# Cross-attention of a decoder layer: how the score maxima reach the rows of the queries

## What is computed

```python
q = (x @ Wq).reshape(B, N, HEADS, hd).transpose(0, 2, 1, 3)      # 16 heads of 32
k = (context @ Wk).reshape(B, M, HEADS, hd).transpose(0, 2, 1, 3)
v = (context @ Wv).reshape(B, M, HEADS, hd).transpose(0, 2, 1, 3)
scores = jnp.einsum('bhid,bhjd->bhij', q, k) * scale
scores = jnp.where(context_mask[:, None, None, :], scores, max_neg)
attn = jax.nn.softmax(scores, axis=-1)
out = jnp.einsum('bhij,bhjd->bhid', attn, v)
```

## Time and profile before

| | us |
|---|---|
| median of 3 runs | 3772.2 (3767.72 to 3776.98) |
| the profiled execution's own time | 3775.88 |
| its span, first to last instruction | 3774.1 |
| TensorE busy | 3639.7 (96%) |
| VectorE busy | 2361.0 (63%) |
| ScalarE busy | 1731.9 (46%) |
| GpSimd busy | 1305.9 (35%) |

### The profile page before, as it was taken

The page is one execution under the profiler, slowest core; times in us unless marked ns, Lnnn a source line. Parts: engine busy times, 40 slices in busy tenths (PEclk is TensorE's granted clock), DMA queues, the critical chain, the costliest instruction groups (busy, mean ns, idle before and its releaser), DMA issues. The chain is left out here.

```text
span 3774.1 us, 84215 instructions
## 1 busy us (share of the span) xinstructions
PE 3639.7 (96%) x28244; PEld 3139.7 (83%) x28244; DVE 2361.0 (63%) x5543; ACT 1731.9 (46%) x4278; POOL 1305.9 (35%) x1388
## 2 busy tenths in 40 slices
PE   8999999999979999999999999849999999999999
PEld 7888888888868888888888888638998899989998
DVE  6888888888846666666666666576433434434343
ACT  4555555555435555555555555413333333333332
POOL 2333333333325656666556566510101101011010
PEclk9999999999989999999999999869999999999999
DMA  4222222222243434444434343223324334234232
GB/s 127 60 54 63 54 63 53 64 53 64 72 122 94 112 106 104 108 116 107 121 96 113 104 108 97 71 68 94 121 82 122 107 98 123 82 118 123 85 108 69
DMA packets 315057, 349.72 MB, mean 93 GB/s; under 512 B 45308, under 2 KB 232036, under 8 KB 314884
## 3 DMA queue, kind: packets, MB, share of 16 engines
q1 hardware_dynamic: 305796, 318.26, 30.7%
q0 software_dynamic: 9088, 29.17, 2.4%
HBM read 183.23 MB, written 38.91 MB: 59 GB/s over the span
## 5 line engine op out<-in xcount | busy, mean ns | idle before, releaser
L1627 DVE TENSOR_REDUCE x_mx<-x_psS 112x1 f32<-112x752 f32 x512 | 479.7, 937 | 382.2 <-PE x_psS L1180 378.6
L2423 DVE TENSOR_TENSOR hid<-e_psU,act_g 128x280 f32<-128x280 f32 x256 | 115.1, 450 | 622.6 <-PE e_psU L34 585.8
L1462 ACT ACTIVATE x_pt<-x_psE 125x448 f32<-125x448 f32 x768 | 389.6, 542 | 227.6 <-PE x_psE L1192 217.7
L1051 POOL TENSOR_TENSOR part<-x_pt 125x448 f32<-125x448 f32 x255 | 292.4, 1147 | 506.0 <-ACT x_pt L1462 497.1
L2049 POOL DMA_INDIRECT out<-ex_y,sidx x40 | 39.8, 995 | 1020.4 <-DVE ex_y L2457 1010.2
L635 POOL TENSOR_TENSOR qks<-qks,cos 128x448 f32<-128x448 f32 x128 | 148.1, 1157 | 657.0 <-DMA qks<-qk 657.0
L1180 PE MATMUL x_psS<-k_st,q_st 97*112 97x376 f32 x1024 | 287.9, 362 | 24.1 <-DMA k_st<-mk 16.3
L32 PE MATMUL e_psG<-ex_hi,g_hi 128*128 128x280 f32 x1024 | 304.2, 297 | 6.7 <-ACT act_g L2208 4.5
L32 PE MATMUL pj<-xT_hi,win_hi 128*128 128x224 f32 x1024 | 302.2, 295 | 4.0 <-PEq L185 3.9
L2208 ACT ACTIVATE act_g<-e_psG 128x280 f32<-128x280 f32 x256 | 103.7, 405 | 426.4 <-PE e_psG L34 412.1
L1053 POOL TENSOR_TENSOR part<-part,x_pt 125x448 f32<-125x448 f32 x255 | 292.3, 1146 | 20.0
(11 more groups left out here) (305 smaller groups left out, 10890.3 us busy)
## 6 DMA issues: line engine op xcount, KB each, us to landing
k_st<-kT SPq DMA_DIRECT2D x768, 93.8 KB, 2.2
raw_g<-in_L_ffn_wg SPq DMA_DIRECT2D x128, 256.0 KB
raw_u<-in_L_ffn_wu SPq DMA_DIRECT2D x128, 256.0 KB
raw_d<-in_L_ffn_wd SPq DMA_DIRECT2D x128, 256.0 KB
qks<-qk SPq DMA_DIRECT2D x512, 56.0 KB, 2.0
q_st<-qT SPq DMA_DIRECT2D x384, 56.0 KB, 2.0
ctxt<-in_ctx SPq DMA_DIRECT2D x16, 1125.0 KB
xt<-in_x SPq DMA_DIRECT2D x16, 448.0 KB, 3.7
```

The lines of the kernel that those rows point to most:

```text
L1051: pool.tensor_tensor(part[:], pt[j][:, 0, :], pt[j][:, 1, :], ALU.add).then_inc(parted, 1)
L1462: act.activation(pt[j][:, i, :], psE[(j + i) % 2][0:KR, 0:2 * T], ACT.Exp, scale=XD ** -0.5).then_inc(exp_done, 1)
L1627: dve.tensor_reduce(mx[:, j, h:h + 1], psS[0:HT, :, 0:376], AX.XY, ALU.max).then_inc(s_taken, 1)
L2423: dve.tensor_tensor(h[ring][:, halves[s]], psU[:, 0:CH], act_g[i][:, halves[s]], ALU.mult).then_inc(S["mul"], 1)
```

## The change

VectorE splits the maxima where they stand (`split_max`), two instructions on 112 x 4 for a pair, right after `maximum` of its last head: a rounded negative high part, and the remainder. One transposition on TensorE turns the eight columns into 8 rows of 112. ScalarE copies them to m_row and issues a DMA from its own queue, which lays them down in rows 97 and 98 of q_st; it waits first for the previous one to land, and for its own copy. TensorE waits for the landing (m_placed) where it waited for the bank. Row 96 keeps the ones that an earlier stage wrote. Pair 0 moves from `first_gap` at j = 3 to the end of `second_gap` at j = 2, which on ScalarE is ahead of the exponentials of j = 3; pair 1 moves to the head of the next group, ahead of everything of it on TensorE and ScalarE. On VectorE the split of pair 0 comes before the residual and `low_k` at j = 1, that of pair 1 after the last maximum; `low_q(b, 3)` and `low_ctx(b, 2, 0)` move from after `maximum(3, 0)` to before it. Two short fills of GpSimd at the start go.

```diff
-UNITS = ("K10 V04 M1_0 K11 Q2 V05 Q3 M0_0 X0 X1 "
-         "K20 V10 M1_1 K21 V11 V12 V13 N0 M0_1 N1 O0 L "
-         "K30 M1_2 O1 K31 V14 V15 C00 C10 Q0 C20 M0_2 C01 Q1 C11 "
-         "K00 C21 V00 M1_3 K01 V01 V02 V03 M0_3").split()
+UNITS = ("M1_0 K10 V04 K11 Q2 V05 Q3 M0_0 X0 X1 "
+         "M1_1 K20 V10 K21 V11 V12 V13 N0 M0_1 N1 O0 L "
+         "M1_2 K30 O1 K31 V14 V15 C00 C10 Q0 C20 M0_2 C01 Q1 C11 "
+         "M1_3 K00 C21 V00 K01 V01 V02 V03 M0_3").split()
...
-            less = sb(c, "x_less", [P, 1])
+            m_parts, m_row = sb(c, "m_parts", [HT, 2, 8], F32R), sb(c, "m_row", [8, HT], F32R)
...
+            def max_placed(t, i):
+
+                return 32 * t + 16 * i + 16
+
+            fills = [ones[:]] + [k[96:99, :].bitcast(F32) for k in k_st]
...
                     def turn_max(u, t, i):
 
-                        pe.wait_ge(s_taken, 8 * t + 4 * i + 4)
+                        pe.wait_ge(m_split, 4 * t + 2 * i + 2)
                         o = bank(u)
-                        for n in range(4):
-                            m = pe.transpose(o[:, n * HT:(n + 1) * HT], mx[:, 2 * i + n // 2, n % 2:n % 2 + 1].to_broadcast((HT, P)),
-                                             ident[0:HT, 0:HT])
-                        m.then_inc(pj_full, 1)
+                        pe.transpose(o[0:8, 0:HT], m_parts[:, i, :].bitcast(F32), ident[0:HT, 0:HT]).then_inc(pj_full, 1)
...
                             elif j == 3:
-                                turn_max(U(f"M0_{g}"), n, 0)
                                 if g == 0 and not last:
...
-                                if prev:
-                                    turn_max(U(f"M1_{g}"), n - 1, 1)
                                 if g == 2 and not first:
                                     project_out(U("O1"), b - 1, 1)
...
                                 elif g == 3 and not last:
                                     project_v(U("V03"), 0, 3)
+                                turn_max(U(f"M0_{g}"), n, 0)
...
+                            if prev:
+                                turn_max(U(f"M1_{g}"), n - 1, 1)
                             for j in range(4):
                                 pe.wait_ge(k_placed[j], placed(b, g))
                                 scores(n, g, j, 0)
                                 if prev:
-                                    if j == 0:
-                                        done(U(f"M0_{gp}") if g else unit_of(b - 1, "M0_3"))
-                                    elif j == 2:
-                                        done(U(f"M1_{g}"))
+                                    if j in (0, 2):
+                                        pe.wait_ge(m_placed, max_placed(n - 1, j // 2))
                                     shifted(n - 1, gp, j, (0, 1))
...
-                    def high_max(u, g, i):
-
+                    def out_max(u, t, g, i):
+
+                        if i or not below(t, 1):
+                            act.wait_ge(m_placed, max_placed(t, i) - 16)
                         o = full(u)
-                        act.activation(q_st[96:99, 4 * g + 2 * i:4 * g + 2 * i + 2, :],
-                                       o[96:99, 0:2 * T].rearrange("p (j t) -> p j t", j=2), ACT.Identity,
-                                       bias=ident[96:99, 96:97], scale=ident[96:99, 98:99]).then_inc(m_high, 1)
+                        act.activation(m_row[:], o[0:8, 0:HT], ACT.Copy).then_inc(pj_free[u.bank], 1)
+                        act.wait_ge(pj_free[u.bank], u.after)
+                        head = 4 * g + 2 * i
+                        act.dma_start(q_st[97:99, head:head + 2, :].bitcast(F32), m_row[:].bitcast(F32)).then_inc(m_placed, 16)
...
                                 elif g == 3 and not last:
                                     out_v(U("V03"), 0, 3)
+                                out_max(U(f"M0_{g}"), t + g, g, 0)
...
                             n, prev = t + g, not (first and g == 0)
+                            if prev:
+                                out_max(U(f"M1_{g}"), n - 1, (g + 3) % 4, 1)
                             for j in range(4):
                                 if prev:
                                     exps(n - 1, j, range(3) if j == 3 else (0, 1))
...
-                    def low_max(u, n, g, i):
-
-                        dve.wait_ge(m_high, n)
-                        rows = q_st[96:99, 4 * g + 2 * i:4 * g + 2 * i + 2, :]
-                        dve.scalar_tensor_tensor(rows, pj[u.bank][96:99, 0:2 * T].rearrange("p (j t) -> p j t", j=2),
-                                                 less[96:99, 0:1], rows.bitcast(F32), ALU.mult, ALU.add).then_inc(pj_free[u.bank], 1)
+                    def split_max(t, i):
+
+                        raw, hi, lo = (mx[:, 2 * i:2 * i + 2, :], *(m_parts[:, i, k:k + 4].rearrange("p (j h) -> p j h", j=2) for k in (0, 4)))
+                        dve.wait_ge(s_taken, 8 * t + 4 * i + 4)
+                        dve.tensor_scalar(hi, raw, -1.0, None, ALU.mult).then_inc(m_split, 1)
+                        dve.wait_ge(m_split, 4 * t + 2 * i + 1)
+                        dve.scalar_tensor_tensor(lo, raw, -1.0, hi.bitcast(F32), ALU.mult, ALU.subtract).then_inc(m_split, 1)
...
-                                if g == 0:
-                                    low_q(b, 3)
                                 if pprev:
                                     out_y(n - 2, (g + 2) % 4, U("O1") if g == 2 and not first else None)
-                                if g == 2 and not last:
-                                    low_ctx(b, 2, 0)
-                                low_max(U(f"M0_{g}"), 2 * n + 1, g, 0)
...
                             elif j == 1:
+                                split_max(n, 0)
                                 if g == 2 and not first:
                                     residual(U("O1"), b - 1, 1)
...
                                 if g == 2 and not last:
                                     low_q(b, 0)
+                                if g == 0:
+                                    low_q(b, 3)
+                                elif g == 2 and not last:
+                                    low_ctx(b, 2, 0)
                             else:
+                                split_max(n, 1)
```

More of the change, by code:

```diff
@@ L966, in place_k @@
                         if below(t, 1):
-                            sp.wait_ge(zeroed, 1)
+                            sp.wait_ge(filled, len(fills))
                         for j in range(4):
@@ L1037, in _ @@
                 def _(pool):
[L1039 to L1042, removed]
+                    for n, f in enumerate(fills):
+                        pool.memset(f, 1.0).then_inc(filled, 1)
                         pool.wait_ge(filled, n + 1)
-                    pool.nop().then_inc(zeroed, 1)
                     def sum_blocks(t, g, heads=range(4)):
@@ L1235, in _ @@
                     pe.wait_ge(rw_out, 1)
-                    pe.wait_ge(zeroed, 1)
+                    pe.wait_ge(filled, len(fills))
                     pe.wait_ge(wo_loaded, 16)
@@ L1246, in first_gap @@
                         def first_gap(g, j):
-                            n, nxt, ng = t + g, not (last and g == 3), (g + 1) % 4
+                            nxt, ng = not (last and g == 3), (g + 1) % 4
                             if j < 2 and nxt:
@@ L1269, in second_gap @@
                         def second_gap(g, j):
-                            n, prev, pprev = t + g, not (first and g == 0), not (first and g < 2)
+                            n, pprev = t + g, not (first and g < 2)
                             if j == 0:
@@ L1350, in _ @@
                     n, last = 4 * B, lambda name: unit_of(B - 1, name)
-                    done(last("M0_3"))
+                    turn_max(last("M1_4"), n - 1, 1)
+                    pe.wait_ge(m_placed, max_placed(n - 1, 0))
                     shifted(n - 1, 3, 0, range(3))
-                    turn_max(last("M1_4"), n - 1, 1)
                     totals(n - 2, 2)
@@ L1357, in _ @@
                     turn_rows(last("N1_14"), B - 2, 1)
-                    done(last("M1_4"))
+                    pe.wait_ge(m_placed, max_placed(n - 1, 1))
                     shifted(n - 1, 3, 2, range(3))
@@ L1504, in first_gap @@
                             elif j == 3:
-                                high_max(U(f"M0_{g}"), g, 0)
                                 if g == 0 and not last:
@@ L1513, in second_gap @@
                         def second_gap(g, j):
-                            gp, prev = (g + 3) % 4, not (first and g == 0)
                             if j == 0:
@@ L1522, in second_gap @@
                                     out_v(U("V00"), 0, 0)
-                                if prev:
-                                    high_max(U(f"M1_{g}"), gp, 1)
                             elif j == 1:
@@ L1576, in _ @@
                     n = 4 * B
-                    exps(n - 1, 0, range(3))
```

(17 more changed lines are left out.)

8 lines of the change are left out of this document (4 added, 4 removed).

## The result

The kernel is slower. The changed kernel's median is 3823.3 us and the old one's, measured beside it, 3775.75, five runs each; the ratio is 1.0126, with a 95% interval of 1.0111 to 1.0141. One disturbed run of 4985.91 us is outside that ratio. The difference of the medians is 47.55 us, of the two profiled spans 45.9 (3774.1 and 3820.0). The forecast was 3809, by a sum of +37.2.

The account below looks back on a forecast made before the run. TensorE bounds the kernel, busy 1294.07 of 1320 us, with ScalarE without slack at j = 3. M0 +49.0, M1 -17.2 and VectorE +5.4 sum to +37.2 us: 3809 as a median, range 3768 to 3838.

Parts of the forecast that it names:

- The issue holds up ScalarE: Each maxima step adds 1.16 us on ScalarE, 0.82 of it DMA issue in which it can start nothing; chance 0.70.
- The rival of a free issue: Issue costs ScalarE nothing or under some 0.2 us: about -1 us, 3771, no measurable difference; chance 0.14.
- the dearer one: SyncE and ScalarE hold each other up, issue 1.21 us: +25 us, 3834; within the blocked queue's 0.70.
- The waits at j = 3: At a group's last head TensorE waits for ScalarE before the third pair, 0.6 to 1 us, some 60 times.
- M1 moved ahead: Pair 1's step at the next group's head: 0.23 us gained 63 times, plus a 2.7 us bank wait; -17.2 us.
- VectorE's moves: Two small VectorE operations of about 0.17 us each delay O1's residual; low_q and low_ctx moves mostly hidden; +5.4 us.
- V15: TensorE unit at g = 2, j = 1 taking its bank after the residual: 0.36 us later, 15 times, +5.4 us.
- The landing: ScalarE's rows land in 2.0 us, before TensorE wants them: no wait; rival of late landing 3863, chance 0.02.
- The term for M0: Pair 0's step ahead of the last head's exponentials delays TensorE 3.12 us a batch over 16 batches: +49.0 us.
- The faster rival: Issue free, removed TensorE transpositions gained: 27 us (3745), or 37 us if all 384 count (3735); chance 0.14.

Follow-up runs that it names:

- the run without it: Changed kernel with VectorE's split moved behind O1's residual: 3812.03 us, 11 us less than the changed kernel.

## Why the prediction was right in sign, and where its sum was off

- **The issue holds up ScalarE: right, and dearer than the rest of the step.** It takes 0.62 us where I took the mask row's 0.82; the exponentials start 1.03 us after the copy's start, not 1.16. As the copy also starts 0.10 us ahead of the recorded end of the instruction before it, the exponentials start 0.93 us after that (1773.35 - 1772.42), 0.23 less than the sum had. That accounts for the 0.2 us by which g = 0 came out below it, and for half of the 0.4 of g = 3. The rival of a free issue is out (in none of the 128 issues does ScalarE start an instruction), and so is the dearer one: 107 of the 128 run while SyncE issues too, and their median is 624 ns like that of the 21 others; a single one lasts 1.50 us. The Trainium skill (DMA: Bandwidth & Descriptors, "Issuing engines are not separate DMA queues") has the time to initiate a DMA as usually small against the DMA; 0.62 us of issue against the 2.0 us in which SyncE's mask row lands is not small, and on a compute engine with no slack it was two thirds of the 0.93; to move it alone gave back as much as to move the whole step.
- **The waits at j = 3: right.** Forecast were waits of 0.6 to 1 us some 60 times; there were 71 with 46.5 us in total, 0.92, 0.40, 0.82 and 0.55 us at the four groups of one batch.
- **M1 moved ahead: right per place.** A single transposition pushes TensorE on by 1777.49 - 1777.46 = 0.03 us where four took 0.31, so 0.28 each instead of 0.23.
- **"VectorE's moves": this step failed.** It looked at O1's residual and V15 alone, and not at what the new place of M1_2 in UNITS does to the units behind it. K30 took O0's bank: 16.8 us of waits. The run with only O0's residual earlier gave 17 us back, and that with M1 and the order in their old places took the same waits away.
- **V15 was undersized.** Forecast +5.4; 11.6 us of waits, and 11 us came back in the run without it. The two operations of the split were taken at 0.17 us each. They last up to 1.1 us (below).
- **The landing: no wait in the changed kernel, as forecast**, but with little room: as soon as M0 is issued behind the exponentials it is waited for, and beside the loads at g = 0 the last packet ends 3 to 5 us after the issue's start, in the changed kernel too. The 2.0 us of the mask row did not hold there.
- **The sum.** In a batch: 2.38 forecast, less four times the 0.23 of the shorter step, plus K30's 1.20 and V15's 0.77 - 0.36, makes 3.07; measured 3.12. With M1's gain at 0.28 it makes 2.87, and 0.25 us a batch have no place, most of it at g = 1. The term for M0, 49.0 us, stands against 42.2 us more of waits for ScalarE; what moving M0 back gives is another matter (the last point). The forecast of 3809 came as near as it did by luck: a step that was too dear (some 15 us over all) hid most of one that was forgotten. The clock in the last three groups, some 10 us by estimate, stands in no term of it.
- **What undoing it gives back.** I had held the M0 places for worth 30 to 42 us if freed. They gave 9 (8.9 and 9.3 in the 15 batches), since the exponentials' turnaround of 1.01 us, the maximum of the last head and the landing are each only a little behind the issue. The faster rival's 27 to 37 us for the transpositions were thus never there: 12 in the old kernel.

What stays open: what sets the clock in the last three groups, why g = 1 lost as much as forecast though the step was shorter, and 8 of the 86 us of the doubled issue in the batches.

## What to carry to other kernels

A DMA issued from a compute engine's queue costs that engine its whole issue (0.62 us here): put it behind what the bound engine waits for, and look then what comes next, since three limits within half a microsecond of each other give back far less than the first one's waits. Where buffers are handed round by the order of a list, an entry that is moved changes whose buffer each entry behind it inherits: go through all of them, with who frees each. And cost removed work at zero where another engine's turnaround already sets the distance. Compare two profiles stage by stage, with the granted clock beside each, before a difference is given to the change.

## What the runs showed of the hardware that was not expected

**Small VectorE operations that begin under one of GpSimd's last until that is over.** The 128 pairs of the split in the changed kernel, ns minimum, median, maximum:

```profile
L1632 DVE TENSOR_SCALAR m_parts<-x_mx x128: 169/459/807, 1100.7 to 2469.0; 112x4 fp32r<-112x4 f32 x128
L1634 DVE SCALAR_TENSOR_TENSOR m_parts<-x_mx,m_parts x128: 161/164/1103, 1100.9 to 2469.3; 112x4 fp32r<-112x4 f32 x128
```

One such case on GpSimd and on VectorE:

```profile
1785.91 1.15 POOL L1054 TENSOR_TENSOR part<-x_pt 125x448 f32<-125x448 f32 x1 [0.25 <-POOL x_lnw L1075]
```

```profile
1785.81 0.17 DVE L1632 TENSOR_SCALAR m_parts<-x_mx 112x4 fp32r<-112x4 f32 x1
1786.01 1.06 DVE L1634 SCALAR_TENSOR_TENSOR m_parts<-x_mx,m_parts 112x4 fp32r<-112x4 f32 x1
```

GpSimd's ends at 1787.06, VectorE's, begun 0.10 us after it, at 1787.07. The one that ran ahead of it took 0.17. At V15 it was the first that was caught:

```profile
1831.60 0.63 DVE L1632 TENSOR_SCALAR m_parts<-x_mx 112x4 fp32r<-112x4 f32 x1
```

with GpSimd's operation from 1831.05 to 1832.20. It holds for all: of the 128 first operations 99 last over 0.2 us; each of these began while a GpSimd operation ran and ended 0.02 to 0.03 us after its end. None of the other 29 began under one of GpSimd's operations of 0.2 us or more. Of the second ones 14 are long, and all 14 end so. The row of 112x2 from which I took 0.17 us had never met more than the last 0.04 us of one; in the changed kernel 15 of the 16 begin under one, and the median is 1.10 us (169/1095/1119 ns). The Trainium skill (SBUF — State Buffer, "SBUF: two separate sides") says that VectorE and GpSimd share a pair of ports under an exclusive lock for a whole instruction, where VectorE's has two inputs in SBUF or runs in a 2-port mode. The trace agrees for L1634, which has two; L1632 has one, and no row tells its mode.

**The clock.** Over the 15 batches the kernel with 128 more issues, and so more and longer waits of TensorE (the longest 1.9 us), was granted 0.97 and the changed kernel 1.00. Idle time grew by 42 us, the time by 86: a wait of TensorE's can cost more than its length.
